# Reading TensorE's transposes as the one-pass 32-bit type, in a kernel of local attention and a mixture of experts

## The reference

```python
# attention, 8 heads of 32, blocks of 12 queries that see 24 keys (their block and the 12 rows before)
q, k, v = xn @ Wq.T, xn @ Wk.T, xn @ Wv.T           # q scaled by softplus(per_dim_scale), k by a constant
logits = einsum(q_blocked, k_ctx) + rel_shift(einsum(q_blocked, rel_k))
attn = softmax(tanh(logits / 50) * 50)
out = (attn @ v_ctx) @ Wpost.T
# experts, 8 of hidden size 704, the best two per token
normed = rmsnorm(xn) * norm_weight
probs = softmax(normed @ router_weight.T); top 2, renormalised
out_e = (silu(normed @ gate_e.T) * (normed @ up_e.T)) @ down_e.T
moe = sum over e of combine[:, e] * out_e           # times clip(alpha, -0.5, 2)
```

## Time and profile before

| | us |
|---|---|
| median of 3 runs | 862.78 |
| lowest and highest | 861.61, 870.28 |
| the profiled execution | 869.74 |
| its span, first to last instruction | 867.9 |
| PE busy in the span | 807.0 (93%) |
| DVE, ACT, POOL busy | 439.1, 388.7, 400.3 |

### The profile page before, as it was taken

How to read it: one execution, slowest core, us unless ns; L and a number is a source line. 1 busy time by engine, 2 the same in 40 slices (tenths; PEclk the granted TensorE clock), 3 DMA queues, 4 the chain that set the end, 5 groups by cost and what they waited for, 6 DMA issues and landing times.

```text
span 867.9 us, 19555 instructions
## 1 busy us (share of the span) xinstructions
PE 807.0 (93%) x6503; PEld 776.1 (89%) x6503; DVE 439.1 (51%) x1037; ACT 388.7 (45%) x663; POOL 400.3 (46%) x304
## 2 busy tenths in 40 slices
PE   0678999999999999989999999999999999999994
PEld 0668999999999999888999999999999999999993
DVE  3625236777888544434444444444444444444442
ACT  4266558877666678722222332223222233222330
POOL 1138566777857566722333333333433333333332
PEclk9969689999999999979999999999999999999998
DMA  9515865988876443210236355255264363222211
GB/s 280 201 56 188 283 220 180 297 278 290 271 247 201 129 143 109 62 33 19 38 65 186 78 134 145 38 139 140 38 164 116 67 177 82 35 38 37 35 26 23
DMA packets 69217, 114.77 MB, mean 132 GB/s; under 512 B 11640, under 2 KB 52516, under 8 KB 69124
## 3 DMA queue, kind: packets, MB, share of 16 engines
q0 software_dynamic: 18304, 39.47, 17.8%
q1 hardware_dynamic: 34692, 44.66, 17.2%
q10 hardware_dynamic: 16128, 29.36, 11.8%
HBM read 66.57 MB, written 46.93 MB: 131 GB/s over the span
## 4 chain that ended last, share of the span: by engine, by line
PE 68%; POOL 10%; ACT 8%; issue 7%; DVE 3%; ACTq 2%; DMA 2%; SPq 0%; POOLq 0%; DVEq 0%
PE psum L1117 58%; POOL w_ring L523 5%; PE psum L1206 5%; POOL arena L557 4%; ACT psum L711 2%; PE psum L1172 2%; PE psum L1265 2%; ACT arena L687 2%; ACT arena L715 1%; PE psum L1133 1%; DMA out<-spare,sca_i 1%; ACT w_ring L651 1%; ACTq L629 1%; DMA arena<-xn_all 1%; POOL arena L515 1%
## 5 line engine op out<-in xcount | busy, mean ns | idle before, releaser
L1117 PE MATMUL psum<-w_ring,xT 128*128 x1608 | 276.1, 327 | 3.9 <-DVE xT L1005 3.7
L1117 PEld LDWEIGHTS psum<-w_ring,xT 128*128 128x128 f32 x1608 | 257.0, 188 | 15.4 <-issue 15.4
L570 POOL DMA_INDIRECT out<-spare,sca_i x67 | 106.6, 1590 | 281.3 <-DVE spare L1104 261.8
L1117 PE MATMUL psum<-w_ring,hT 128*128 x1139 | 152.7, 288 | 1.9 <-DVE spare L1104 1.4
L996 DVE TENSOR_TENSOR spare<-psum,spare 128x704 f32<-128x704 f32 x67 | 59.7, 891 | 164.6 <-PE psum L1117 164.6
L1117 PEld LDWEIGHTS psum<-w_ring,hT 128*128 128x128 f32 x1139 | 140.6, 190 | 2.3 <-issue 2.3
L759 ACT ACTIVATE spare<-psum 128x704 f32<-128x704 f32 x67 | 50.8, 758 | 159.9 <-PE psum L1117 159.9
L668 ACT ACTIVATE xT<-psum,nwp 128x128 fp32r<-128x128 f32 x134 | 41.9, 363 | 172.4 <-PE psum L1172 169.8
L557 POOL TENSOR_TENSOR arena<-arena,const 120x540 f32<-120x540 f32 x38 | 64.4, 1694 | 103.5 <-ACT arena L715 103.5
L1117 PE MATMUL psum<-arena 32*120 32x108 f32 (+1 forms) x1216 | 92.1, 281 | 0.0
L1117 PEld LDWEIGHTS psum<-arena 32*120 32x120 f32 (+1 forms) x1216 | 84.1, 185 | 8.8 <-issue 1.0
(11 more groups left out here) (161 smaller groups left out, 994.5 us busy)
## 6 DMA issues: line engine op xcount, KB each, us to landing
w_split<-w_ring POOLq DMA_DIRECT2D x20, 1088.0 KB, 8.0
w_ring<-w_split SPq DMA_DIRECT2D x40, 544.0 KB
raw<-in_w_raw ACTq DMA_DIRECT2D x32, 544.0 KB, 4.9
nrm_d<-x_all ACTq DMA_DIRECT2D x8, 512.0 KB, 5.5
arena<-xn_d SPq DMA_DIRECT2D x34, 120.0 KB
arena<-in_x SPq DMA_DIRECT2D x37, 108.0 KB
out<-arena SPq DMA_DIRECT2D x37, 108.0 KB
bd_d<-arena SPq DMA_DIRECT2D x38, 84.4 KB
```

The source lines that it names most:

```text
L570: pool.indirect_dma_start(out=out, out_offset=bass.IndirectOffsetOnAxis(ap=sca_i[:, b:b + 1], axis=0), in_=y[:, b % 2, :], in_offset=None, ...
L1117: return pe.matmul(out_ap, lhs, rhs, start=first, stop=last)
```

## The change

Every transpose now reads its data and its identity or permutation as F32R, and writes PSUM through a view of the same type. For that, the program lays F32R views over the same bytes (`xg_m`, `xn_m`, `arena_m` with `win_m`, `o_m`, `spread_m`, and `hb_m`), and a new tile `turns` holds copies of the identity and of both permutations in this type. DVE makes the two copies right at its start, after a wait for the constants, and PE waits for them before its first transpose. The number, the shapes and the order of the transposes are unchanged.

```diff
+        turns = sb("turns", [P, P + 2 * GK], F32R)
+        xg_m = sb("xg_m", [P, NXG, D], F32R, at=xg_at)
+        ident_m = turns[:, 0:P]
+        perm_in = turns[0:GK, P:P + GK]
+        perm_out = turns[0:GK, P + GK:P + 2 * GK]
...
             link(dve.memset(rel_bd[:, :, :, :], 0.0))
+            dve.wait_ge(s_const, 16)
+            dve.tensor_copy(ident_m, ident).then_inc(s_turns, 1)
+            dve.tensor_copy(turns[:, P:P + 2 * GK], const[:, C_IN:C_IN + 2 * GK]).then_inc(s_turns, 1)
 
             dve.wait_ge(s_dim, 16 * HC)
...
+            def moved(out_ap):
+                return out_ap.bitcast(F32R)
...
-                        ins = pe.transpose(psum[:, 4, D + k * P:D + (k + 1) * P], xn_all[:, t, k * P:(k + 1) * P], ident)
+                        ins = pe.transpose(moved(psum[:, 4, D + k * P:D + (k + 1) * P]), xn_m[:, t, k * P:(k + 1) * P], ident_m)
...
-                    ins = pe.matmul(psum[:, 2, k * GK:(k + 1) * GK], win[0:GK, window(g), k * P:(k + 1) * P], perm_in,
+                    ins = pe.matmul(moved(psum[:, 2, k * GK:(k + 1) * GK]), win_m[0:GK, window(g), k * P:(k + 1) * P], perm_in,
                                     start=True, stop=True, is_transpose=True)
...
-                    ins = pe.transpose(psum[:, x_bank(b), k * P:(k + 1) * P], xg[:, b % NXG, k * P:(k + 1) * P], ident)
+                    ins = pe.transpose(moved(psum[:, x_bank(b), k * P:(k + 1) * P]), xg_m[:, b % NXG, k * P:(k + 1) * P],
+                                       ident_m)
...
-                    ins = pe.transpose(psum[:, 4 + c // 3, (c % 3) * P:(c % 3 + 1) * P], hb[:, b % 2, c * P:(c + 1) * P],
-                                       ident)
+                    ins = pe.transpose(moved(psum[:, 4 + c // 3, (c % 3) * P:(c % 3 + 1) * P]),
+                                       hb_m[:, b % 2, c * P:(c + 1) * P], ident_m)
...
-                        pe.matmul(psum[0:GK, i, k * GQ:(k + 1) * GQ],
-                                  spread[0:GQ, HC * k + i, :, :, :].rearrange("p a r n -> p (a r n)"),
-                                  ident[0:GQ, 0:GQ], start=k == 0, stop=False, is_transpose=True)
+                        pe.matmul(moved(psum[0:GK, i, k * GQ:(k + 1) * GQ]),
+                                  spread_m[0:GQ, HC * k + i, :, :, :].rearrange("p a r n -> p (a r n)"),
+                                  ident_m[0:GQ, 0:GQ], start=k == 0, stop=False, is_transpose=True)
...
-                    ins = pe.matmul(psum[:, 6, k * GK:(k + 1) * GK],
-                                    o_sb[0:GK, HC * k:HC * (k + 1), :].rearrange("p h n -> p (h n)"), perm_out,
+                    ins = pe.matmul(moved(psum[:, 6, k * GK:(k + 1) * GK]),
+                                    o_m[0:GK, HC * k:HC * (k + 1), :].rearrange("p h n -> p (h n)"), perm_out,
                                     start=True, stop=True, is_transpose=True)
...
             pe.wait_ge(s_const, 16)
+            pe.wait_ge(s_turns, 2)
             turn(0)
```

More of the change, by code:

```diff
@@ L135, in program @@
         in_use = sb("in_use", [1, 2], I32)
+        xg_at = cursor[0]
         xg = sb("xg", [P, NXG, D])
@@ L142, in program @@
         mask = const[0:GK, C_MASK:C_MASK + GQ]
-        perm_in = const[0:GK, C_IN:C_IN + GK]
-        perm_out = const[0:GK, C_OUT:C_OUT + GK]
+        turns = sb("turns", [P, P + 2 * GK], F32R)
[3 more added lines that the diff above has]
+        perm_out = turns[0:GK, P + GK:P + 2 * GK]
         ring_at = cursor[0]
@@ L154, in program @@
         xn_all = sb("xn_all", [P, TT, D], at=ring_at)
+        xn_m = sb("xn_m", [P, TT, D], F32R, at=ring_at)
         x_all = sb("x_all", [P, TT, D], at=ring_at + 2 * 2 * WC * 4)
+        spare_at = cursor[0]
         spare = sb("spare", [P, 15, D])
@@ L168, in program @@
         arena = sb("arena", [P, sum(sizes.values())])
-        at, off = {}, 0
+        arena_m = sb("arena_m", [P, sum(sizes.values())], F32R, at=arena_at)
+        at, at_m, off = {}, {}, 0
         for name, n in sizes.items():
             at[name] = arena[:, off:off + n]
+            at_m[name] = arena_m[:, off:off + n]
             off += n
         win = at["win"].rearrange("p (b d) -> p b d", b=NWIN + 1)
+        win_m = at_m["win"].rearrange("p (b d) -> p b d", b=NWIN + 1)
+        o_m = at_m["o"].rearrange("p (h n) -> p h n", h=H)
+        spread_m = at_m["rep"].rearrange("p (h a r n) -> p h a r n", h=H, a=2, n=CHUNK)
         xw = at["xw"].rearrange("p (b d) -> p b d", b=NXW)
@@ L195, in program @@
         hb = spare[:, 6:12, :].rearrange("p t n -> p (t n)")[:, 0:2 * HIDP].rearrange("p (b n) -> p b n", b=2)
+        hb_m = sb("hb_m", [P, 2, HIDP], F32R, at=spare_at + 6 * D * 4)
         y = spare[:, 12:14, :]
@@ L219, in program @@
         s_const = sem("s_const")
+        s_turns = sem("s_turns")
         s_dim = sem("s_dim")
```

## The result

The changed kernel took 877.21 us (median of four runs, 876.14 to 886.82) against 863.60 for the kernel before (four runs, 861.61 to 870.28): 1.0169 times, 95% interval 1.0108 to 1.0231. It is slower, where 845.8 us were forecast and slower had a chance of 0.06. The profiled execution of the changed kernel took 876.51 us, its span was 874.6. In the ratios here, executions more than 1.5% above the fastest of their kernel are left out, which are mostly those with the lowest mean clock, so a ratio can understate what the clock costs.

The account below looks back on a forecast made before the run. TensorE was taken to bound the kernel, chiefly in the expert stage's block loop. 15.3 + 2.3 + 0.9 - 1.5 = 17.0 us off 862.8 gave 845.8 us; range 831 to 865, the forecast's own 836 to 857.

Parts of the forecast that it names:

- What a transpose costs: On TensorE, a 128-column transpose was to start every 80 ns instead of 110, 29 ns less.
- the bounds of 56 and 115: Limits for the changed transpose: 56 ns with one pass on both sides, 115 ns if the weight load paces it.
- Expert transposes, 15.3 us: Expert stage: eight transposes per block, 29 ns less each, save 0.232 us a block over 66 blocks.
- The chain behind them does not change: Expert block: the chain of about 2.0 us to `xT` was to keep its length, so the 0.232 us counts fully.
- Score transposes, 2.3 us: Attention: eight per step save 0.18 us, counted in 13 steps; GpSimd's loop hides it in the others.
- Router transposes, 0.9 us gained, between 0 and 3: Early attention steps: half of 64 router transposes at 29 ns less each was counted as gain.
- I have not split the path between TensorE and the weight pieces: Early attention steps: the stated reason for counting only half of the router transposes' saving, 0.9 us.
- The term that was put at nothing: The sum has no clock term; the granted clock, 1.00, is named for the expert stage. Windows and outputs were put at nothing.
- the one slower rival, a lost transposing path: Each transpose becomes an ordinary 32-bit matmul, 230 ns in place of 110: about 950 us, chance 0.06.
- The copies, 1.5 us: Kernel start: DVE's copies wait for the constants, delaying the query-scale chain 2.3 us; 1.5 us lost, ends 0 and 2.5.
- the case that the loads are bound by their own transfer: Kernel start: less of the copies' delay, perhaps below 0.8 us, passes on if transfer limits the large input loads.

Follow-up runs that it names:

- e8: Changed kernel with F32R transposes in the experts only, copies on GpSimd, ACT's register load moved ahead of its wait: 846.18 us, 0.9699 times the kernel before.
- e10: Kernel before, all transposes plain, with only ACT's register load moved ahead of its wait: 856.67 us, 0.9820 times the kernel before.
- e2: Changed kernel with the expert transposes plain F32 again, F32R in attention only: 885.69 us, 1.0197 times the kernel before.
- e4: Whole change, but GpSimd makes the two copies and DVE does not wait for the constants: 876.35 us, 1.0045 times the kernel before.
- e1: Changed kernel with attention's four kinds of transposes plain F32 again, F32R in the experts only: 864.40 us, 0.9946 times the kernel before.
- e13: Changed kernel unaltered, run again as yardstick beside e14: four runs of 868.60, 882.39, 891.78 and 896.53 us.
- e3: Changed kernel with all transposes plain F32; only DVE's wait and two unread copies stay: 869.65 us, 0.9959 times the kernel before.
- e9: e8 plus F32R transposes of windows, scores and outputs from group 8 on: 837.62 us, 0.9659 times the kernel before.
- e7: Whole change with the router's and windows' F32R transposes issued twice: four runs of 866.15, 867.49, 886.44 and 889.66 us, beside a kernel before of 874.59.
- e14: e7 repeated beside the unaltered whole change: four runs of 880.23, 880.78, 887.75 and 897.96 us, 1.0238 times the kernel before.

## Why the prediction was wrong

**What a transpose costs.** Right. 78 ns from start to start, where 80 were taken between the bounds of 56 and 115, and the load record stayed at 140 ns. That it came so close is in part luck: the point between the bounds, a quarter of the way up from the 71 ns of the one-pass matmul, was chosen and not worked out. The Trainium skill ("TensorEngine Tiling (Array Packing)", Restrictions) names one transpose mode for FP32 and FP32R input. It states no pace for it. The trace agrees as far as the load goes, whose record is 140 ns in both types; the moving side, 110 against 78 ns, is not the same.

**Expert transposes, 15.3 us.** The term was 7.3 us (a block went from 6.98 to 6.87 us over all 67). The transposes gave 0.25 us a block, where 0.232 was worked out, but "The chain behind them does not change" was false: the register load in it went from 278 to 406 ns, which leaves 0.12 against 0.11 measured. The runs with the load out of the chain (e8, e10) confirm that it stood in it. What slows the load was not tried. In the kernel before it begins 0.02 us before the end of DVE's multiply of the block (504.44 against 504.46), in the changed one 0.26 us before it (502.48 against 502.74), and in the other blocks of the two traces likewise; in e8 and e10, where the load runs beside no such multiply, it takes 278 and 277 ns. A contention between the two fits all of this and is only argued.

**Score transposes, 2.3 us.** From the ninth tanh to the last it was 0.9 us less, but that is no measure of the term: the same stretch took 223.8 to 236.6 us in the other profiles (236.6 in e10, with plain transposes). The steps without tables kept their distance, as forecast. Those with tables came some 0.1 us closer together, where 0.2 was forecast, but for the first of them, which grew from 9.22 to 10.53 us.

**Router transposes, 0.9 us gained, between 0 and 3.** Here the prediction failed. "I have not split the path between TensorE and the weight pieces" was the place where the front of the kernel was passed over, and with it the clock. The prediction names the granted clock for the expert stage only, where it is 1.00; for the stretch from 50 to 150 us the windows of the kernel before say 0.81 and 0.87, so this stretch changed between the two levels already. The term that was put at nothing is the one for the clock: in the eight early steps it fell from 0.86 to 0.68, and they took 15.1 us more, with the transposes shorter as forecast. No rival had the clock in it, and the one slower rival, a lost transposing path, did not happen: the 0.06 for slower was given for a reason that was not the one at work.

What the runs show in its place: with all four kinds of one-pass transposes in attention's early steps the clock there is lower (0.63 on average in e2 and e4 between 50 and 150 us, 0.90 without them in e1), and the steps are longer in the same measure. Length times clock of the eight steps is 69 to 70 us in the whole change, e2 and e4, at clocks of 0.67 and 0.68 (66 in e13, at 0.59), and 75 to 77 in the kernel before, e1, e3, e8, e9 and e10, at 0.86 to 0.96. The wait for the constants has no part in it that can be told (e3, e4). Why shorter transposes lower the clock stays open: the doubled transposes (e7, e14) raised it in the profiled steps and did not bring the time back in the second trial.

**The copies, 1.5 us.** DVE's chain for the query scale began at 7.29, where 7.6 was forecast:

```profile
6.96 0.23 DVE L808 CAST turns<-const 128x128 fp32r<-128x128 f32 x1 [5.89 <-DMA const<-in_const]
7.10 0.28 DVE L809 CAST turns<-const 128x240 fp32r<-128x240 f32 x1
7.29 0.15 DVE L812 TENSOR_SCALAR q_scale<-q_scale 128x1 f32<-128x1 f32 x1
```

but little of the 2 us was passed on. The issue of the last large load of `x` ended at 13.14 in place of 12.43, ACT's first normalised rows began at 15.12 in place of 14.40 and TensorE's first transpose at 22.46 in place of 21.98; nothing of it was left at the first tanh. So the term was at its lower end, which is where the prediction had put the case that the loads are bound by their own transfer.

## What to carry to other kernels

Read the granted clock in every stretch before forecasting that a shorter TensorE instruction shortens the kernel: here a stretch that already changed between the two levels lost some 20 us by the lower one where its shorter instructions gained some 5, and the stretch at 1.00 beside it told nothing of that. Where several engines pass a block around, list the sequencer's instructions in the chain as well, such as a register load behind a wait; moved ahead of the wait, the load alone brought the kernel to 0.982 times, where the change of type, in the experts alone, had brought it to 0.995. And make such a change by stages, since its sign can differ from one stage to the next.

## What the runs showed of the hardware

A 128-column transpose of 32-bit data started every 110 ns as plain F32 and every 78 ns as F32R at 2.4 GHz, with the same load record of 140 ns. A plain F32 projection of 128 loaded columns had a distance that about doubled at the lower level of the clock (16 of them in 1.94 and in 3.73 us). The reading of one register from SBUF on ACT took 278 or 406 ns (medians), by where in the block it fell. And one unchanged kernel's time follows its clock: on one chip (beside e1 to e4), the kernel before took 860.85 us in an execution with a mean granted clock of 0.978, and 882.54 us in one with 0.956.
